# Attention: a unit's last value products issued in the next unit's first steps, its division job one step earlier; the first experts' first weight row made by TensorE

## The reference

```python
def _gqa(x, ...):                      # x: 4 sequences... flattened below: B, S = 1, 2048
    q, k, v = ...                      # 16 heads, k and v repeated 4 times
    scores = einsum('bhqd,bhkd->bhqk', q, k) / sqrt(8)
    attn = softmax(scores, axis=-1)
    out = einsum('bhqk,bhkd->bhqd', attn, v)
    return out @ ow + ob
def _moe(x, gate_w, w1, w2):           # top 2 of 8 experts by sigmoid(x @ gate_w), capacity 640
    w_topk = w_topk / (sum(w_topk) + 1e-6)
    h = gelu(einsum('ecd,edf->ecf', padded_x, w1))
    out_padded = einsum('ecf,efd->ecd', h, w2)
    ...                                # each token's outputs, times its weights, summed
src = rmsnorm(x + _gqa(x)); src = src + _moe(src); return rmsnorm(src)
```

## Time and profile before

| | |
|---|---|
| median of 3 runs | 2082.84 us (2080.17 to 2083.97) |
| the profiled execution | 2082.48 us |
| its span | 2080.8 us |
| its mean granted TensorE clock | 0.92 |
| busy: PE / DVE / ACT / POOL | 1735.3 (83%) / 1350.4 (65%) / 1168.6 (56%) / 289.8 (14%) us |
| chain that ended last, by engine | PE 54%, DVE 30%, ACT 8%, issue 3%, DMA 3%, POOL 1% |
| its largest line | DVE MX L1097 17% |
| attention stage | about 347 to 1044 us of the span |
| first experts, from wtT on | about 1090 to 1217 us |

### The profile page before, as it was taken

One profiled execution on the slowest core, in us unless ns is written; L12 is line 12 of the kernel. 1 busy time (PEld: TensorE's weight loads), 2 busy tenths in 40 slices (PEclk: granted clock), 3 DMA queues, 4 the chain that ended last, 5 costly groups with the idle time before them and its releaser, 6 DMA issues.

```text
span 2080.8 us, 28060 instructions
## 1 busy us (share of the span) xinstructions
PE 1735.3 (83%) x10350; PEld 791.3 (38%) x10350; DVE 1350.4 (65%) x2649; ACT 1168.6 (56%) x2128; POOL 289.8 (14%) x384
## 2 busy tenths in 40 slices
PE   5898067799999999999848958999888997399998
PEld 3887064122222222222233423444444443244443
DVE  6998876999999899999043354665566655222222
ACT  5565004388888888888833336665566664222222
POOL 3465002200000000000010020111111111111110
PEclk8999577699999999999969978999999999599999
DMA  1000000212000000000104300000000000122420
GB/s 49 1 1 1 0 1 8 58 19 37 2 2 2 2 2 1 2 2 2 32 12 86 91 16 0 16 16 7 10 16 16 16 0 1 49 37 40 60 54 27
DMA packets 76653, 41.19 MB, mean 20 GB/s; under 512 B 22144, under 2 KB 72832, under 8 KB 76528
## 3 DMA queue, kind: packets, MB, share of 16 engines
q1 hardware_dynamic: 75952, 38.75, 9.5%
q10 hardware_dynamic: 576, 0.79, 0.1%
HBM read 36.17 MB, written 3.15 MB: 19 GB/s over the span
## 4 chain that ended last, share of the span: by engine, by line
PE 54%; DVE 30%; ACT 8%; issue 3%; DMA 3%; POOL 1%; SPq 0%; DVEq 0%; ACTq 0%; POOLq 0%
DVE MX L1097 17%; PE PS L1585 6%; PE PS L1153 5%; PE PS L1591 5%; PE PS L2017 4%; PE PS L2018 4%; PE PS L2027 4%; PE PS L1179 3%; ACT tmpb L1223 3%; PE PS L1536 3%; PE PS L523 3%; DMA SB<-scr_w 3%; PE PS L1555 2%; PE PS L1427 2%; PE PS L1420 2%
## 5 line engine op out<-in xcount | busy, mean ns | idle before, releaser
L1223 ACT ACTIVATE tmpb<-PS 128x512 f32<-128x512 f32 x1024 | 553.9, 595 | 100.3 <-PE PS L1179 83.9
L1097 DVE TENSOR_REDUCE MX<-PS 128x2 f32<-128x1024 f32 x512 | 585.9, 1218 | 33.6 <-PE PS L1079 29.7
L1153 PE MATMUL PS<-tmpb,VS 128*32 128x256 f32 x4096 | 327.8, 395 | 14.0 <-ACT tmpb L1223 6.6
L1079 PE MATMUL PS<-KST,QST 56*128 56x512 bf16 x1024 | 206.5, 402 | 22.2 <-DVE MX L1097 21.1
L1179 PE MATMUL PS<-QST,KST 59*128 59x512 bf16 x1024 | 201.8, 391 | 18.0 <-ACT tmpb L1223 15.8
L2052 DVE TENSOR_TENSOR HG<-HG,PS 128x512 f32<-128x512 f32 (+1 forms) x96 | 65.9, 686 | 199.7 <-PE PS L2018 199.7
L2042 ACT ACTIVATE HG<-PS 128x512 f32<-128x512 f32 (+1 forms) x96 | 57.2, 595 | 208.2 <-PE PS L2017 208.2
L1153 PEld LDWEIGHTS PS<-tmpb,VS 128*32 128x32 f32 x4096 | 82.9, 109 | 177.1 <-issue 83.8
L1179 PEld LDWEIGHTS PS<-QST,KST 59*128 59x128 bf16 x1024 | 49.2, 93 | 240.5 <-ACT tmpb L1223 227.5
L1585 PE MATMUL PS<-X,WF 128*128 128x512 f32 x256 | 128.3, 636 | 4.2 <-ACT X L1730 4.2
L1746 ACT ACTIVATE HF<-PS,CL 128x512 f32<-128x512 f32 x128 | 88.0, 687 | 68.6 <-PE PS L1585 68.6
(11 more groups left out here) (313 smaller groups left out, 2553.3 us busy)
## 6 DMA issues: line engine op xcount, KB each, us to landing
SB<-scr_w SPq DMA_DIRECT2D x16, 1024.0 KB, 15.1
WF<-in_L_attn_Wf SPq DMA_DIRECT2D x16, 256.0 KB, 3.0
QST<-NMP SPq DMA_DIRECT2D x192, 1.0 KB
G<-in_L_ffn_w SPq DMA_DIRECT2D x16, 176.0 KB, 2.4
W<-in_L_ffn_w SPq DMA_DIRECT2D x16, 128.0 KB, 2.1
QST<-scr_q SPq DMA_DIRECT2D x14, 128.0 KB
scr_q<-tmpb SPq DMA_DIRECT2D x3, 512.0 KB, 3.6
KST<-scr_k SPq DMA_DIRECT2D x14, 96.0 KB
```

Source lines behind the costliest of these rows:

```text
L1079: pe.matmul(PS[:, b + x, :], QST[r, 2 * g + jj, CH * qc + P * t:CH * qc + P * t + P], KST[r, g, cs(kc)], start=True, stop=True).then_inc(s ...
L1097: r = v.tensor_reduce(MX[:, :, m // (TPC * NC), m // NC % TPC, m % NC], PS[:, b:b + 2, :], AX.X, ALU.max)
L1153: last = pe.matmul(PS[32 * j:32 * j + 32, 3, h], VS[:, kt, u // NC, :], PB[:, kt % 2, j, h], start=(kt == 0 and half == 0), stop=(kt == NT ...
L1223: a.activation(PB[:, kt % 2, j, :], PS[:, at % 3, :], ACT.Exp, scale=HD ** -0.5).then_inc(s_exp, 1)
```

## The change

In attention, the loop's last value products are no longer issued behind the unit's loop. In key tile 0's two steps of the next unit, where there were no value products, TensorE issues half 0 and half 1 of the last unit's last key tile; for the last unit they follow the whole loop. The "values" job moves from step 3, ahead of the max job, to step 2, behind the max job.

In the first experts, the sums of line 1410 become `pe_sums0` and go ahead of the routing's matmuls. Expert 0's row is no longer read back by DMA: `pe_row0` multiplies wtT with one column of the identity, repeated 128 times as the stationary operand, for each of the 16 token tiles, into banks 4 to 7; ScalarE copies banks 4 and 6, VectorE banks 5 and 7, into SB's buffer 0. `pe_moe0` waits for all four copies. Row 1 and all later ones come by DMA as before. `v_weights` counts the four new increments of `s_tr` for the second router.

```diff
         def ahead(u, i):
             jobs = []
-            if i == 3 and u:
-                jobs.append(("values", u - 1))
             v, m = u + 1 + (i + EARLY) // UM, (i + EARLY) % UM
             if v < NU:
                 jobs.append(("max", v, m))
+            if i == 2 and u:
+                jobs.append(("values", u - 1))
...
                     if kt:
                         pe_values(pe, u, kt - 1, jj)
-                pe_values(pe, u, NT - 1, 0)
-                pe_values(pe, u, NT - 1, 1)
+                    elif u:
+                        pe_values(pe, u - 1, NT - 1, jj)
+            pe_values(pe, NU - 1, NT - 1, 0)
+            pe_values(pe, NU - 1, NT - 1, 1)
             pe_job(pe, ("values", NU - 1))
...
-            for k in range(2):
-                sp_row(sp, r, k, k)
+            sp_row(sp, r, 1, 1)
...
-        def pe_moe0(pe):
-            pe.wait_ge(R0["s_pd"], 1)
+        def pe_sums0(pe):
             for c in range(NC):
                 pe.matmul(PS[:, c, :], ident[:, :], HT[:, cs(c)], start=True, stop=False, skip_group_check=True)
             pe.sem_inc(s_hfree, 4)
+
+        def pe_row0(pe, r):
+            pe.wait_ge(r["s_pd"], 1)
+            for c in range(NC):
+                for j, t in enumerate(tiles(c)):
+                    last = pe.matmul(PS[:, 4 + c, P * j:P * j + P], ident[:, E0 * t:E0 * t + 1].to_broadcast([P, P]), r["wtT"][:, :],
+                                     start=True, stop=True)
+                last.then_inc(r["s_tr"], 1)
+
+        def act_row0(a, r, c):
+            a.wait_ge(r["s_tr"], 1 + c + 1)
+            a.activation(SB[:, 0, ts_(c), :].rearrange("p t n -> p (t n)"), PS[:, 4 + c, :], ACT.Copy).then_inc(s_sb0[0], 4)
+
+        def v_row0(v, r, c):
+            v.wait_ge(r["s_tr"], 1 + c + 1)
+            v.tensor_copy(SB[:, 0, ts_(c), :].rearrange("p t n -> p (t n)"), PS[:, 4 + c, :]).then_inc(s_sb0[0], 4)
+
+        def pe_moe0(pe):
+            pe.wait_ge(s_sb0[0], 4 * NC)
             with pe.Fori(0, E0 // 2):
...
             act_route0(a, R0)
+            for c in (0, 2):
+                act_row0(a, R0, c)
             act_moe0(a)
...
             pe_router(pe, R0, 3 * NC, 16)
+            pe_sums0(pe)
             pe_route0(pe, R0)
+            pe_row0(pe, R0)
             pe_moe0(pe)
...
             v_route0(v, chain, R0)
+            for c in (1, 3):
+                v_row0(v, R0, c)
             v_moe0(v)
```

More of the change, by code:

```diff
@@ L1298, in v_weights @@
         def v_weights(v, chain, r):
-            v.wait_ge(r["s_tr"], r["nth"])
+            v.wait_ge(r["s_tr"], r["nth"] + (NC if r["nth"] > 1 else 0))
             chain.link(v.tensor_copy(r["wtT"][:, :], PS[:, 5, 0:P]))
```

## The result

| | before | after |
|---|---|---|
| median of the runs, us | 2082.01 (2080.17 to 2083.97, 4 runs) | 2045.41 (2045.15 to 2045.70, 4 runs) |
| profiled execution, us | 2082.48, span 2080.8 | 2045.65, span 2043.9 |
| mean granted clock | 0.92 | 0.923 |
| ratio after / before | | 0.9824, 95% interval 0.9807 to 0.9841 |

What follows compares the result with a forecast made beforehand. VectorE was taken to bound attention, losing idle time at unit boundaries. 26.6 + 3.8 + 1.0 + 6.4 = 37.8 us off the profiled 2082.48 gives 2044.7, as median 2045.0; range 2036 to 2060.

Steps and rivals of the forecast that it cites:

- 14 boundaries: Attention unit boundaries with maxima beside them: VectorE's idle 1.26 and 0.60 us go, 1.9 us each, 26.6 us in all.
- last boundary: Attention's last unit boundary, without VectorE and bound by ScalarE: unit 15's thirteenth exponential comes 3.8 us sooner.
- clock dip: Clock of 0.66 at one attention boundary (725 to 730), making a unit 41.2 instead of 40.2 us: 1.0 us gone.
- first row: First experts: row by TensorE instead of DMA brings the third second-layer product 6.4 us sooner; ends 2.9 to 8.4.
- The row job's 0.33: Attention: VectorE's 0.33 us idle time after the row job's copy (NMP) in each unit stays.
- The rows' landing: Unit start: negative maxima's DMAs land at most 1.02 us after last issue, by 761.80, needed 762.01; cover 0.2 + 0.3 us.
- Nothing is given back: First experts: the next pair's row 2, about 12 us, shifts with the loop, so the first row's gain is kept.
- A new stall in step 2: Rival, attention: TensorE's wait for PV leaves VectorE idle about 1.0 us a boundary; gain 23.8 us, 2059; chance 13%.
- Late rows: Rival, unit start: rows land only at 763.5, so 1.26 us stays and only 0.6 goes; 2063; chance 5%.
- Weight loads not hidden: Rival, first row: loads between the 32 passes, 10.0 us; part gains 1.7 instead of 6.4; 2050, half clock 2060; 4%.
- Maxima lengthened by TensorE's writing: Rival ("Slower"), attention: PSUM writes lengthen each of 512 reductions; beyond 0.074 us each the kernel is slower; chance 4%.
- More than I say: Rival, later expert blocks: the four slow of eight may all turn fast (-6.6), with a warm row (-2): 2036; 8%.

Runs made afterwards that it cites:

- mx_short: Kernel after, with the maxima taken over 448 of each bank's 512 columns, leaving out 64 keys per bank: 2032.45 us, ratio 0.9764.
- rows_last: Kernel after, with TensorE's row job behind the step's value products instead of ahead of them: 2042.98 us, ratio 0.9810.
- job_only: Kernel before, with only the division ("values") job moved from step 3 to step 2: 2076.58 us, ratio 0.9968.
- row_only: Kernel before, with only the first experts' part (row by TensorE, sums ahead of the routing, copies), no attention edits: 2073.45 us, ratio 0.9965.
- sums_only: Kernel before, with only the four sums moved ahead of the routing; the row still comes by DMA: 2080.57 us, ratio 0.9995.
- late4: Kernel after, with the row job one step later, moving SP's twelve DMAs by about 1.1 us: 2059.10 us, ratio 0.9897.
- after_again: The kernel after once more, unchanged, in the same group as best: 2043.99 us, ratio 0.9819.
- split: Kernel after, with the first experts' first W1 product waiting only for the copy of its own bank 4: 2046.60 us, ratio 0.9827.
- warm: Kernel after, with three filler products on TensorE between the routing's small product and the row's passes: 2045.56 us, ratio 0.9833.
- best: Kernel after, with rows_last, warm and split in one: 2042.03 us, ratio 0.9807.
- values_only: Kernel before, with only the last value products moved; the division job stays in step 3: 2056.60 us, ratio 0.9887.
- attn_only: Kernel before, with both attention edits and nothing of the first experts' row: 2051.14 us, ratio 0.9854.

## Why the prediction was right, step by step

| term | forecast, us | measured, us |
|---|---|---|
| 14 boundaries | 26.6 | 26.5 (14 x 1.89) |
| last boundary | 3.8 | 3.2 |
| clock dip | 1.0 | 1.9 |
| later start of the stage | none | -0.6 |
| first row | 6.4 | 5.4, and 0.2 ahead of wtT |
| sum | 37.8 | 36.6 at the third W2 product, 36.9 in the span |

**What bounds.** Confirmed, with a limit. That VectorE sets a unit's length was read from its runs of 17 maxima without a gap. The units became shorter by about the idle time taken from VectorE, and mx_short shortened them further. But the next engine is 0.77 us a unit behind, and from the row job at 735.75 to the maximum at 750.6, 15 of the unit's 38.3 us, the chain of the kernel after already runs through TensorE and ScalarE and not through VectorE.

**The boundaries.** 1.86 to 1.94 was worked out by carrying the old durations through the new order, 1.9 taken, and 1.89 came. Of its steps: scores 0 were to go right behind the value products, and do; the wait for PV was put at 0.43 us and is 0.38; ScalarE's pause at "about 0.4" is 0.67; the transposes, at 0.60, take 0.63. One step was off: the maximum behind the division was to be written 0.13 us ahead of its use, and VectorE waits 0.33 instead of the old 0.15, 0.18 more, since TensorE is late with it (rows_last, above); job_only shows the same idle time (0.36) without the other edit. That 1.9 still fits has a second reason that the working had not counted: within a piece reductions follow one another at 1.139 us, but a piece's last one takes its full 1.215. With each of the two idle times 0.08 us of that goes as well (11 in one piece take 12.54 us, 8 and 3 took 9.14 + 3.49). 1.26 + 0.60 + 0.16 - 0.18 = 1.84, against 1.89.

**The row job's 0.33** was said to stay, and stayed, in rows_last too, where I had expected it gone.

**The last boundary.** The thirteenth exponential of unit 15, at 1012.91, was forecast 3.8 us nearer, beyond the shift of the stage. ScalarE in order of time, after:

```profile
978.57 32.04 ACT L1225 ACTIVATE tmpb<-PS 128x512 f32<-128x512 f32 x58 [0.66 <-PE PS L1179]
```

The seventh exponential at 978.57 and six more at 0.55 give 981.9, 31.0 us sooner than 1012.91. The last maximum had moved by 27.8, so 3.2 are left. 0.2 of the 0.6 missing are ScalarE's pause (0.66 instead of 0.4); the rest arose ahead of the boundary.

**The clock.** The dip of the earlier trace rows is gone: no boundary of the kernel after has one. What I had missed is a second unit of the kernel before, 41.80 us long (maxima from 565.37 and 607.17):

```profile
585.20 0.22 DVE L1103 TENSOR_REDUCE MM<-MX 128x16 f32<-128x64 f32 x1 [0.50 <-DVE MX L1097]
...
590.00:595.00 5.00, 5.00 (x48) 1.01 (x40) 3.52 (x5) 3.21 (x6) 0.00 (x0) 0.76 0.02 5
```

This dip doesn't stand at a boundary. It begins at 589, at the row job and 29 us into the unit, after TensorE has waited 0.72 and 0.83 us there for VectorE's maxima. The unit's first 0.35 us too many are those ahead of MM, which row_only and sums_only have in the same unit without a dip (40.53 us), and the kernel after too (38.65); the dip itself cost 1.3 us. With the 1.0 of the earlier trace rows, and small differences between units, 1.9 came out. But the change leaves the wait at the row job in place (0.42 and 0.83 us in the same unit of the kernel after, without a dip), so those 1.3 us can't be credited to it. That TensorE's pause at the boundary brings dips there is borne out by count, not shown by a run made for it: the four profiles that keep the pause ahead of step 0 (before, job_only, row_only, sums_only) have four dips behind 56 boundaries, the ten others none behind 140. In late4 TensorE waits up to 0.9 us at each boundary, without a dip.

**How near the sum came.** That the time lies within 0.4 us of the one predicted is in part luck. The boundaries were right to 0.1 us. The last boundary, the start of the stage and the first row together fell 2.2 us short, 0.2 came ahead of wtT, and 0.9 more than forecast came by the clock, of which 1.3 us had been a dip that the change doesn't bear on. Executions of one kernel also differ by more than 0.4 us.

**The rows' landing.** The bound of 1.02 us behind the last issue is met: 1.60 less the issue's 0.57 is 1.03. The forecast had "0.2 + 0.3 us" of cover; late4 shows 0.2. The 0.3 was what VectorE was thought to have in hand. It isn't there: between the row job and the division the chain runs through TensorE, so that a delay of TensorE's scores delays the unit.

**The first row.** The step that was mis-sized: "half clock for the first 16 passes and full for the rest", 5.7 us. It was 6.34; with 0.236 and 0.120 us a pass that is some 22 passes at half clock (32 x 0.120 = 3.84; 2.50 over, by 0.116 each). after_again had 14 (5.43 us), row_only and split about 25. One execution can't size this term better than that, 0.9 us between two executions of the same kernel, and the ends named, 3.9 and 7.6, were the right way to put it. The four sums cost nothing, but only just: they take 6.41 us, from 1048.53 to 1054.94, where a mixture near 5.5 was called likely, and the routing's small product follows at 1055.10. It takes 0.40 us at the full clock (1.00) instead of 0.61 at half (0.50): that is the 0.2 ahead of wtT. "Nothing is given back" holds but for 0.6 us: the next pair's row took 13.17 us instead of 12.55.

**The rivals.** A new stall in step 2: no, 0.18 us instead of 1.0. Late rows: no, but by 0.2 us. Weight loads not hidden: no. warm, with 32 passes that each load one repeated column, 3.65 us of loads within 3.85 us, has them hidden. The Trainium skill's rule (TensorE: Matmul & The Clock Gate, Part 3, "What overlaps and what doesn't"), by which loads and matmuls of the same row groups don't overlap, isn't borne out here: by it the 32 passes would take about 10 us, as the rival put it, and not 3.85. Maxima lengthened by TensorE's writing: no, 1214 ns against 1218. "More than I say": the later expert blocks alternate between about 5.4 and 3.9 us in the kernel after too, four slow ones of eight as before, so nothing came of it; best, split and sums_only show that other patterns occur, and why the blocks alternate stays open.

## What to carry to other kernels

Where several engines carry nearly the same load, find the one without gaps, list its idle times in one period, and ask of each which instruction ends it; work moved in another engine's order that takes such an idle time away is worth about its length times the number of periods (here 1.89 us a period for 1.86; the smaller edit alone 0.49 for 0.60, since it opened a new wait), until the next engine is reached, and here that was 0.8 us further. Before counting on more, move the neighbouring job by one step or shorten the bounding instruction a little: that measures the cover and the lead. A broadcast of a few kilobytes that waits for DRAM and back can be made by matrix products with a repeated column, where TensorE is idle anyway and the banks are free; here that gave 5.4 us.

## What the runs showed of the hardware

- Sixteen or 32 fp32 passes of 128x128, each with weights of its own: 0.120 us a pass at full clock (warm), 0.236 at half, the loads (0.19 us each) hidden at full clock (3.65 us of loads within 3.85 us, warm).
- The same 32 passes behind the same routing took 5.43, 6.34, 6.70 and 6.75 us in four executions: the instant at which the full clock comes differs by some 10 passes from one to the next.
- The 1 KB DMAs between SBUF tiles, issued by SP each 0.61 us, land 1.60 us after the start of the last issue (late4).
- The later expert blocks' first eight products take 5.4 to 5.6 us and 3.86 us in turn in most executions. In three profiled ones (sums_only, split, best) this breaks once, with three slow blocks in a row, and costs some 4 us (510.6 to 510.9 us from the first block to the router instead of 506.6 to 506.9); sums_only's and split's profiled executions are also the slowest of their runs, 4.1 and 3.2 us above the median.
- Between 410 and 980 us of the span, where TensorE is busy nearly throughout, the granted clock fell in 5 places in 14 profiles: four behind a boundary with TensorE's pauses of 0.37 to 0.53 us, one behind its waits of 0.72 and 0.83 us at the row job. Seven profiles without the boundary's pauses (values_only, attn_only, after, after_again, late4, warm, split) have the 0.83 us wait at the row job too, and no dip.
